# Chunked attention: causal mask added to two quarters of a chunk, and the first 64 queries' product taken over 64 keys

## The reference

```python
log_f = jax.nn.log_sigmoid(fg)
cs = jnp.cumsum(log_f, axis=-1)
diff = cs[..., :, None] - cs[..., None, :]
mask = jnp.tril(jnp.ones((Sq, Sq), dtype=bool))
log_fg_mat = jnp.where(mask, diff, -jnp.inf)
log_D = log_fg_mat + ig[..., None, :]
max_log_D = jnp.max(log_D, axis=-1, keepdims=True)
D = jnp.exp(log_D - max_log_D)
qk = jnp.einsum('bhsd,bhtd->bhst', qh, kh) / jnp.sqrt(jnp.float32(dh))
C = qk * D
normalizer = jnp.maximum(jnp.abs(C.sum(-1, keepdims=True)), jnp.exp(-max_log_D))
h = jnp.einsum('bhst,bhtd->bhsd', C / (normalizer + EPS), vh)
```

## Time and profile before

| what | value |
|---|---|
| time, median of 3 runs | 3072.02 us (3067.55 to 3075.28) |
| the profiled execution's own time | 3074.24 us |
| its span, first to last instruction | 3072.5 us |
| mean granted TensorE clock | 0.986 |
| TensorE busy over the span | 96% |
| VectorE, ScalarE, GpSimd busy | 60%, 37%, 34% |
| attention, by the rows of its products | up to about 980 us |
| experts | from about 1050 us to the end |

### The profile page before, as it was taken

One profiled execution on the slowest core, in us unless ns is written; L12 is line 12 of the kernel. 1 busy time (PEld: TensorE's weight loads), 2 busy tenths in 40 slices (PEclk: granted clock), 3 DMA queues, 4 the chain that ended last, 5 costly groups with the idle time before them and its releaser, 6 DMA issues.

```text
span 3072.5 us, 60746 instructions
## 1 busy us (share of the span) xinstructions
PE 2964.4 (96%) x24708; PEld 2398.2 (78%) x24708; DVE 1832.6 (60%) x5124; ACT 1138.2 (37%) x2025; POOL 1057.8 (34%) x1028
## 2 busy tenths in 40 slices
PE   6999999999997599999999999999999999999998
PEld 5888888888886477777777777787787777778886
DVE  6999998999998645354454444445435444444322
ACT  5778787877886311121121121122112112112110
POOL 4767687777766211111112111121112111121111
PEclk9999999999998799999999999999999999999999
DMA  3243434434342422231242131232123214222121
GB/s 129 84 166 113 167 135 144 158 121 167 130 149 104 137 42 35 37 99 31 44 100 47 37 79 34 37 95 62 31 37 88 45 31 110 37 49 58 35 37 23
DMA packets 140062, 250.68 MB, mean 82 GB/s; under 512 B 31457, under 2 KB 31457, under 8 KB 139785
## 3 DMA queue, kind: packets, MB, share of 16 engines
q1 hardware_dynamic: 105784, 170.80, 16.5%
q0 software_dynamic: 28672, 67.65, 12.5%
q10 hardware_dynamic: 5328, 8.36, 0.9%
HBM read 137.23 MB, written 101.19 MB: 78 GB/s over the span
## 4 chain that ended last, share of the span: by engine, by line
PE 63%; DMA 2%; DVE 1%; issue 0%; ACT 0%; POOL 0%; ACTq 0%; DVEq 0%; POOLq 0%
PE DN L1710 31%; PE UP L1684 29%; PE TT L1657 2%; DMA w_raw<-in_L_ffn_W_down 2%; DVE c_hit L1380 0%; DVE down_lo L1246 0%; PE c_bank L1373 0%; ACT z L1629 0%; PE c_bank L1357 0%; DVE c_hit L1401 0%; DVE c_within L1396 0%; ACT down_hi L1240 0%; POOL out_x L1604 0%; DVE mid_lo L1742 0%; DVE c_gained L1433 0%
## 5 line engine op out<-in xcount | busy, mean ns | idle before, releaser
L1604 POOL DMA_INDIRECT out_x<-y,slots x128 | 202.0, 1578 | 1640.5 <-DVE y L1764 1640.5
L1710 PE MATMUL DN<-down_hi,mid_hi 128*128 128x512 f32 x1408 | 579.2, 411 | 0.0
L1629 ACT ACTIVATE z<-UP,bup 128x512 f32<-128x512 f32 (+1 forms) x352 | 240.8, 686 | 853.8 <-PE UP L1684 836.9
L1684 PE MATMUL UP<-xT_hi,up_hi 128*128 128x512 f32 (+1 forms) x1408 | 553.1, 393 | 1.9 <-DVE xT_lo L1721 0.9
L1684 PE MATMUL UP<-xT_hi,up_lo 128*128 128x512 f32 (+1 forms) x1408 | 554.8, 394 | 0.0
L1684 PE MATMUL UP<-xT_lo,up_hi 128*128 128x512 f32 (+1 forms) x1408 | 551.3, 392 | 0.0
L1710 PE MATMUL DN<-down_hi,mid_lo 128*128 128x512 f32 x1280 | 505.1, 395 | 0.0
L1710 PE MATMUL DN<-down_lo,mid_hi 128*128 128x512 f32 x1280 | 504.9, 394 | 0.0
L1740 DVE CAST mid_hi<-z 128x512 fp32r<-128x512 f32 (+1 forms) x352 | 151.1, 429 | 484.3 <-ACT z L1629 484.3
L1613 ACT ACTIVATE xT_hi<-TT 128x512 fp32r<-128x512 f32 x126 | 75.1, 597 | 702.9 <-PE TT L1657 682.9
L1684 PEld LDWEIGHTS UP<-xT_hi,up_hi 128*128 128x128 f32 (+1 forms) x1408 | 259.8, 185 | 68.5 <-ACT z L1629 4.5
(11 more groups left out here) (263 smaller groups left out, 5005.3 us busy)
## 6 DMA issues: line engine op xcount, KB each, us to landing
xs<-in_x SPq DMA_DIRECT2D x32, 1024.0 KB, 8.3
kraw<-in_ctx SPq DMA_DIRECT2D x32, 1024.0 KB, 5.7
out_x<-xs SPq DMA_DIRECT2D x32, 1024.0 KB, 12.7
rows_scratch<-xfb SPq DMA_DIRECT2D x32, 1024.0 KB, 10.8
w_raw<-in_L_ffn_W_down SPq DMA_DIRECT2D x40, 512.0 KB, 4.4
w_raw<-in_L_ffn_W_up SPq DMA_DIRECT2D x16, 682.5 KB, 4.1
mid_hi<-mid_hi ACTq DMA_DIRECT2D x32, 86.0 KB
mid_lo<-mid_hi ACTq DMA_DIRECT2D x32, 84.0 KB
```

What stands on the lines that cost most here:

```text
L1604: pool.indirect_dma_start(out_rows, bass.IndirectOffsetOnAxis(ap=slots[:, m:m + 1], axis=0), y[:, t, :], None, compute_op=ALU.add).then_in ...
L1629: act.activation(z[0:r, k % 2, :], UP[k % 3][0:r, :], ACT.Silu, bias=bup[0:r, e // 2, f:f + 1]).then_inc(s["z"], 1)
L1684: mm = pe.matmul(UP[k % 3][0:r, :], weights.up[wa][:, c, f * P:f * P + r], xT[xa][:, c, :], start=first, stop=(c == CH - 1 and wa == 1))
L1710: mm = pe.matmul(DN[m % 2][:, :], lhs, rhs, start=first, stop=(f == FCH - 1 and lhs is parts[-1][0]))
```

## The change

In `decays` the two `climb` products come first and clear the banks; the four mask products follow, each on 4 x 64 columns instead of 512: for keys 0 to 63 the queries 0 to 63 of each chunk, for keys 64 to 127 the queries 64 to 127. The wait for `climb` now stands ahead of both. The quarter of unseen keys is thus no longer masked, and holds whatever the exponential gives there. In `product` the half a = 0 therefore contracts over keys 0 to 63 alone (`seen`), with 64 rows; the half a = 1 still contracts over all 128.

```diff
                     top, end = slice(0, DH), slice(DH, P)
-                    for a, r, mask in ((0, top, (maskneg, maskswap)), (1, end, (maskswap, maskneg))):
-                        for t, m in zip((top, end), mask):
-                            pe.matmul(EX[t, a, :], identb[r, r], m[r, :], start=True, stop=False, skip_group_check=True)
                     if p == 0:
                         pe.wait_ge(s["rp"], b + 1)
                     for a, r in ((0, top), (1, end)):
                         ones_of = pick[r, p, :, :].rearrange("k a j -> k (a j)")
-                        pe.matmul(EX[:, a, :], climb[r, b % 2, :], spread(ones_of, 2, P), start=False, stop=False, skip_group_check=True)
+                        pe.matmul(EX[:, a, :], climb[r, b % 2, :], spread(ones_of, 2, P), start=True, stop=False, skip_group_check=True)
+
+                    for a, r, mask in ((0, top, (maskneg, maskswap)), (1, end, (maskswap, maskneg))):
+                        for t, m in zip((top, end), mask):
+                            own_half = [x.rearrange("k (n t) -> k n t", t=P)[:, :, t] for x in (EX[t, a, :], m[r, :])]
+                            pe.matmul(own_half[0], identb[r, r], own_half[1], start=False, stop=False, skip_group_check=True)
...
                             for a in range(2):
                                 r = slice(DH * a, DH * a + DH)
-                                mm = pe.matmul(A[r, par, j, 0:VW], C[:, 2 * (g % CRING) + par, j * P + DH * a:j * P + DH * a + DH],
-                                               vc[:, b % 2, j, 2 * p + par, :], start=(j == 0), stop=(j == 0), skip_group_check=True)
+                                seen = slice(0, DH * a + DH)
+                                mm = pe.matmul(A[r, par, j, 0:VW], C[seen, 2 * (g % CRING) + par, j * P + DH * a:j * P + DH * a + DH],
+                                               vc[seen, b % 2, j, 2 * p + par, :], start=(j == 0), stop=(j == 0), skip_group_check=True)
```

## The result

The changed kernel took 3738.38 us (median of 4 runs, 3732.84 to 3739.56) against 3073.65 us: 1.214 times as long, 95% interval 1.212 to 1.216. The forecast of slower was right, the time 3510 us and its range up to 3716 were too low. The profiled execution took 3738.1 us, span 3736.4, with a mean granted clock of 0.896 instead of 0.986.

The account below looks back on a forecast made before the run. TensorE, busy 96% of the span, was taken to bound the kernel, with VectorE close behind in attention. The terms: 3074.2 + 390 (product) + 4 (masks) - 18 (waits) + 64 (clock) = 3514, given as 3510 us, range 3344 to 3716.

Parts of the forecast that it names:

- the product, 128 times: Attention's product: 16 alternating-shape instructions at 0.259 us, 4.14 us instead of 1.09, +390 us over 128 products.
- the masks: Decays: halved columns save 0.11 us, but new changes of shape and an exposed load cost more; +4 us together.
- waits that go: Attention: TensorE's iteration gets longer, VectorE's does not, so TensorE's waits for VectorE go; -18 us, between 0 and -22.
- the clock: Attention: some sparse products are followed by a stretch at 1.2 GHz; +64 us, ends none to 192 us.
- the side-by-side rival: Product: 64*64 and 128*64 tiles in disjoint columns run side by side, product stays 1.09 us; 3076 us, chance 0.09.
- the drain to the recorded end: Product's upper bound: each next shape waits until the record before has ended; 5.3 us a product, +538 us.
- one in three: Clock term: 43 of 128 products are followed by a 3.5 us stretch at 1.2 GHz losing 1.5 us, +64 us.
- my mild bound of one fall behind each product: Clock term's upper end: a stretch at 1.2 GHz behind every product, 128 x 1.5 = 192 us; 3640 us.
- A clock that falls far more often: Attention: the clock falls far more often than the forecast took, 3740 us and over; chance 0.04.
- The second window of the earlier trace: At 230 to 234 us TensorE was as idle as at 171 to 175, yet the clock stayed at 1.00.
- The third rival: Clock stays low in all of the sparse product: 7.3 us each, +405 us in place of the 64; 3850 us.

Follow-up runs that it names:

- e1: The kernel before with only the new decays (climb first, masks on 4 x 64 columns), product as before: 3090.56 us, ratio 1.0034.
- e4: The whole change with loops over half and two heads exchanged, 8 changes of shape a product instead of 16: 3291.09 us, 1.069 times the kernel before.
- e5: The whole change with all products of a = 0 first, then all of a = 1: 3185.52 us, 1.034 times the kernel before.
- e12: The whole change with 6 dense 128*64 matmuls added ahead of each product: 3863.32 us, 1.254 times the kernel before.
- e11: The whole change with 6 dense 128*64 matmuls added in the middle of each product: 3501.21 us, 1.137 times the kernel before.
- e7: The kernel before with masks on 4 x 64 columns, still ahead of climb, product as before: 3080.32 us, ratio 0.9999.
- e9: The kernel before with 13 matmuls of 128*128 and only 4 moving columns added ahead of each product: 3813.74 us, ratio 1.239.

## Why the prediction was wrong

Its steps, one by one, against the changed kernel's profiled execution of 3738.1 us:

| step | predicted | measured |
|---|---|---|
| the product, 128 times | +390 us | 128 x (4.12 - 1.08) = +389 us |
| the masks | +4 us | +6 to +15 alone (e1) |
| waits that go | -18 us | all of TensorE's, 22.0 down to 2.7: -19 us |
| the clock | +64 us | the rest: 3738.1 - 3074.2 - 389 - 4 + 19 = +290 us |

**The product's mechanism was right, and its size exact.** Each change of shape costs 0.14 us, with the load; e4 and e5 give it again from other counts of changes. Halving the rows saved nothing, the disjoint columns did not help (the side-by-side rival fell: 4.12 us and single starts), and the switches around the cheaper masks ate their gain, as the rows of before said. Of the bounds, the drain to the recorded end (5.3 us a product) was too dear. The Trainium skill, page "TensorEngine Tiling (Array Packing)", section Key Properties, says that changing the tiling mode drains TensorE. The runs agree that each change costs, 0.14 us here, and less than a wait for the recorded end would (4.12 us a product, not 5.3).

**The step that failed is the clock's:** "I take one in three, 43 x 1.5 = +64 us: the product is not quite as sparse, and dense work stands on both sides of it." By its own terms it allowed 43 stretches of 3.5 us, 150 us at 1.2 GHz; it was 703 us, 4.7 times that: 90 stretches, twice as many, of 7.8 us on average, more than twice as long. The loss for each of these microseconds was well guessed: 290/703 = 0.41, against 1.5/3.5 = 0.43. So it was the amount of low time alone. Even my mild bound of one fall behind each product, 192 us, was below what came, though the falls were fewer than the products: it priced each at 3.5 us. A clock that falls far more often, "3740 us and over", had a chance of 0.04.

The reasons for keeping it small did not hold. Dense work beside a sparse run does not protect the clock (e12); dense work inside it does (e11). The rate of one in three was not too low for the places of the trace of before, but they were another kind of place. The second window of the earlier trace rows is no twin of the first: it begins in a dense product and holds 54 records in 3.4 us, against 27 in 4.0. Moved to where TensorE is sparse it holds 31 in 4.0, and the clock stayed at 1.00 there too. And there is a second fall, behind 33 records in 4.0 us (columns as in the earlier trace rows):

```profile
231.50:235.50 4.00, 3.07 (x31) 2.35 (x29) 2.34 (x7) 2.54 (x6) 3.93 (x4) 1.00 0.02 4
526.50:530.50 4.00, 3.27 (x33) 2.55 (x29) 2.13 (x7) 2.54 (x6) 3.90 (x5) 1.00 0.02 4
530.70:534.10 3.40, 3.40 (x48) 2.98 (x48) 3.22 (x11) 1.61 (x3) 3.24 (x5) 0.50 0.01 2
```

Places of up to 35 records in 4.0 us are at least eight in the attention of before (about 48, 76, 171, 231, 350, 527, 839 and 962 us), with two falls behind them. They are waits and small pieces between dense work, and both low stretches ended after 3.4 us. The new product is 4.1 us of sparse work without a break, 128 times: 90 falls, and low stretches that last 7.8 us.

The third rival, a clock low through all sparse products, had a product at 4.14 x 1.93/1.09 = 7.3 us. One at 1.2 GHz throughout takes 6.50, but only 8 of the 128 were: the clock falls late in a product or behind it, and 589 of the 703 us lie in the work between, which nearly doubles (scores 0.98 to 1.84 us).

With 290 in the clock's place the sum comes to the measured execution, but that shows nothing, since 290 is what the other terms leave. An estimate that does not use it: the 114 us in products made them 42 us longer in all, and the other 589, at the scores' (1.84 - 0.98)/1.84 = 0.47, would lose 275 us; together 317, where 290 were left.

The Trainium skill, page "TensorE: Matmul & The Clock Gate", Part 1, says of the clock that "activity releases the throttle". The runs agree, and show it where no gap is to be seen: in the changed kernel's attention TensorE is busy 1594 of 1597 us by the profile and the clock is at 0.78, and 6 more matmuls in the middle of each product keep it at 0.97 (e11).

## What to carry to other kernels

Neighbouring matmuls that take different rows x columns of the array cost 0.14 us a change here, and lose the side-by-side run of disjoint columns: shrinking one of a pair to half its contraction saves nothing and breaks both, so keep shapes equal, or group them. A shortened operand counts only if it is on the engine's path and opens no new change of shape; e7 removed 14 us of TensorE's time cleanly and gained nothing. And when an edit makes TensorE's work sparse for some microseconds without a break, price the clock for the dense work that follows too: here a fall lasted 7.8 us on average, not the 3.4 us of the few falls before. A few dense matmuls placed inside the sparse run can cost less than they give back.

## What the runs showed of the hardware that I had not expected

- Adding work to a kernel made it faster by 237 us (3738 to 3501) when it broke a sparse run of 4.1 us in two, and slower by 125 us (3863) when it stood ahead of the run.
- Sparse work of 3.0 us a product (e4, 8 changes of shape) left the clock at 1.00; 4.12 us (16 changes) brought it to 0.78. The two differ in length and in records a microsecond; 2.9 us of still thinner work (e9) brought it to 0.74. Where the limit lies I did not look for.
- At 1.2 GHz a product full of shape changes took 6.50 us instead of 4.12 (58% more), and dense scores 1.84 us instead of 0.98 (88% more).
- TensorE was busy 1594 of 1597 us of attention by the profile, while its clock was at 0.78: the busy share does not tell how much the array has to do.
